# A graph network on one core: SyncE waits for the landings of gathers and counts units in place of GpSimd, and a round's weights are loaded after the first body

## The reference

```python
for l in range(L):                                   # L = 3
    agg = segment_sum(h[src], dst, num_segments=N) / deg
    logits = concatenate([h, agg], axis=-1) @ router_W[l] + router_b[l]
    ...                                              # top 2 of 8, softmax
    weak = relu(einsum('nh,ehf->nef', agg, weak_W[l]) + weak_b[l])        # 4 experts
    sh = relu(einsum('nh,ehf->nef', agg, strong_W1[l]) + strong_b1[l])    # 4 experts, 512 wide
    strong = einsum('nef,efh->neh', sh, strong_W2[l]) + strong_b2[l]
    h = h + sigmoid(h @ conf_W[l] + conf_b[l]) * einsum('ne,neh->nh', gate_dense, experts)
```

## Time and profile before

| | busy us | share of the span | instructions |
|---|---|---|---|
| TensorE (PE) | 3301.5 | 55% | 12044 |
| VectorE (DVE) | 3403.5 | 56% | 6527 |
| ScalarE (ACT) | 1200.4 | 20% | 2737 |
| GpSimd (POOL) | 4450.2 | 74% | 4528 |

### The profile page before, as it was taken

One profiled execution on the slowest core, in us unless ns is written; L12 is line 12 of the kernel. 1 busy time (PEld: TensorE's weight loads), 2 busy tenths in 40 slices (PEclk: granted clock), 3 DMA queues, 4 the chain that ended last, 5 costly groups with the idle time before them and its releaser, 6 DMA issues. The chain is left out here.

```text
span 6044.4 us, 58307 instructions
## 1 busy us (share of the span) xinstructions
PE 3301.5 (55%) x12044; PEld 2061.7 (34%) x12044; DVE 3403.5 (56%) x6527; ACT 1200.4 (20%) x2737; POOL 4450.2 (74%) x4528
## 2 busy tenths in 40 slices
PE   6249799999879899989899999100000000000000
PEld 3145455556545555565465555100000000000000
DVE  4136566663556666636566665455555536566563
ACT  1013233333223233323233333100000000000000
POOL 6767777776777777767777775777777777777777
PEclk9559899999789999979999999555555555555555
DMA  2143333333333333333333331122222212222221
GB/s 72 35 134 103 102 104 102 104 102 102 114 103 103 103 103 102 100 118 104 102 103 99 103 97 53 48 55 55 55 55 56 55 51 55 54 55 55 55 55 50
DMA packets 229761, 495.01 MB, mean 82 GB/s; under 512 B 96472, under 2 KB 113039, under 8 KB 229487
## 3 DMA queue, kind: packets, MB, share of 16 engines
q0 software_dynamic: 184432, 463.70, 28.7%
q1 hardware_dynamic: 45188, 29.87, 1.7%
HBM read 462.21 MB, written 31.05 MB: 82 GB/s over the span
## 5 line engine op out<-in xcount | busy, mean ns | idle before, releaser
L545 POOL DMA_INDIRECT ring<-hidden_tab,stage x2400 | 2330.3, 971 | 803.9 <-issue 621.6
L545 POOL DMA_INDIRECT ring<-gat_tab,stage x1600 | 1553.2, 971 | 496.5 <-issue 449.9
L834 DVE TENSOR_TENSOR ps_wide<-ps_wide,ring 128x1024 f32<-128x1024 f32 x450 | 554.7, 1233 | 335.1 <-POOLq L556 214.9
L1734 PE MATMUL ps_w1a<-ident,agg_team_t 128*128 128x128 f32 x28 | 7.8, 435 | 1044.6 <-DVE agg_team_t L1157 1044.6
L1604 PE MATMUL ps_w1a<-agg_team_t,wbuf 128*128 128x512 f32 (+1 forms) x1248 | 561.8, 572 | 7.3 <-ACT strong L1287 5.9
L1629 PE MATMUL ps_gate<-wbuf,strong 128*128 128x256 f32 x2400 | 561.5, 380 | 0.0
L1604 PE MATMUL ps_w1b<-agg_team_t,wbuf 128*128 128x512 f32 (+1 forms) x1248 | 556.0, 568 | 0.0
L1629 PE MATMUL ps_wide<-wbuf,strong 128*128 128x256 f32 x2304 | 537.2, 379 | 0.0
L1629 PEld LDWEIGHTS ps_gate<-wbuf,strong 128*128 128x128 f32 x2400 | 433.5, 191 | 111.6 <-issue 47.7
L1426 ACT ACTIVATE ps_gate<-shifted 128x36 f32<-128x36 f32 x296 | 60.4, 204 | 1959.6 <-DVEq L1068 1952.0
L1629 PEld LDWEIGHTS ps_wide<-wbuf,strong 128*128 128x128 f32 x2304 | 415.3, 190 | 78.5
(11 more groups left out here) (351 smaller groups left out, 4883.5 us busy)
## 6 DMA issues: line engine op xcount, KB each, us to landing
ring<-hidden_tab,stage POOLq DMA_INDIRECT x2400, 2.8
ring<-gat_tab,stage POOLq DMA_INDIRECT x1600, 2.6
hidden_tab<-h_res SPq DMA_DIRECT2D x12, 512.0 KB, 3.0
wbuf<-in_L_gnn_strong_W SPq DMA_DIRECT2D x6, 1024.0 KB, 9.9
wbuf<-in_L_gnn_strong_W SPq DMA_DIRECT2D x12, 512.0 KB, 12.4
wbuf<-in_L_gnn_weak_W SPq DMA_DIRECT2D x6, 512.0 KB, 7.2
stage<-slot_tab SPq DMA_DIRECT2D x125, 16.0 KB, 1.8
slot_tab<-wbuf SPq DMA_DIRECT2D x1, 1584.0 KB, 6.4
```

The lines of the kernel that those rows point to most:

```text
L545: return pool.indirect_dma_start(out=ring[:, b, 0:width], out_offset=None, in_=table, in_offset=bass.IndirectOffsetOnAxis(ap=stage[:, half ...
L834: nc.vector.tensor_tensor(wide_s, wide_s, rows(u), ALU.add).then_inc(ring_free, 1)
```

## The change

SyncE no longer follows `arrived` but makes it. For each body it waits for every unit's landing semaphore and counts the unit (`tell`); GpSimd keeps the wait for a free unit and, with it, an increment of `half_begun`, which nobody reads. Each unit is counted once, so the others wait for `u + 1` in place of `u + (r + 2)`. `round_gathered` is gone. In hidden rounds SyncE now loads the second body's indices, tells all units of the first body, issues the weights, loads the third body's indices and tells the units of the second body.

```diff
             for r in range(LAYERS + 2):
-                if r:
-                    sp.wait_ge(round_gathered, r)
                 def load(m, half):
                     return sp.dma_start(stage[:, half, :], slot_tab[:, bass.ds(m * RING, RING)]).then_inc(staged[half], 16)
-                def next_load(m, half):
+                def tell(m):
                     if r < LAYERS:
-                        sp.wait_ge(arrived, bodies * (UNITS * r) + m * UNITS + (r + 1 - 2 * UNITS))
+                        for u in range(UNITS):
+                            sp.wait_ge(gathered[u], bodies * (16 * SLOTS * r) + m * (16 * SLOTS) + 16 * SLOTS * (2 if u == UNITS - 1 else 1))
+                            sp.sem_inc(arrived, 1)
                     else:
-                        k = r - LAYERS
-                        sp.wait_ge(garrived, bodies * (GUNITS * k) + m * GUNITS + (k + 1 - 2 * GUNITS))
-                    load(m - 1, half)
+                        for u in range(GUNITS):
+                            sp.wait_ge(ggathered[u], bodies * (16 * GSLOTS * (r - LAYERS)) + m * (16 * GSLOTS) + 16 * GSLOTS * (2 if u == GUNITS - 1 else 1))
+                            sp.sem_inc(garrived, 1)
                 sp.dma_start(stage[:, 0, :], slot_tab[:, 0:RING]).then_inc(staged[0], 16)
                 if r == 0:
                     sp.wait_ge(s_slotst_rest, 16)
                 if r < LAYERS:
-                    sp.wait_ge(arrived, bodies * (UNITS * r) + (r + 1))
+                    load(1, 1)
+                    tell(0)
                     if r:
                         sp.wait_ge(w2_ready, r * BATCHES * 2 * NS)
...
-                with sp.Fori(1, bodies // 2 + 1) as j:
-                    next_load(j * 2, 1)
-                    next_load(j * 2 + 1, 0)
+                    load(2, 0)
+                    tell(1)
+                with sp.Fori(1 if r < LAYERS else 0, bodies // 2) as j:
+                    load(j * 2 + 1, 1)
+                    tell(j * 2)
+                    load(j * 2 + 2, 0)
+                    tell(j * 2 + 1)
+                with sp.Fori(bodies // 2, (bodies + 1) // 2) as j:
+                    tell(j * 2)
...
                         if b % SLOTS == SLOTS // 2:
                             pool.wait_ge(ring_free, i * UNITS + (b // SLOTS + 2))
-                            pool.wait_ge(gathered[(b // SLOTS - 1) % UNITS], i * (16 * SLOTS) + 16 * SLOTS)
-                            pool.sem_inc(arrived, 1)
+                            pool.sem_inc(half_begun, 1)
                         gather(b, half).then_inc(gathered[b // SLOTS], 16)
...
-                dve.wait_ge(arrived, first + (r + 2))
+                dve.wait_ge(arrived, first + 1)
```

More of the change, by code:

```diff
@@ L286, in gnn_kernel @@
         staged = [sem(f"staged{h}") for h in range(2)]
-        half_begun, arrived, round_gathered, ring_free, table_done = (sem(n) for n in (
-            "half_begun", "arrived", "round_gathered", "ring_free", "table_done"))
+        half_begun, arrived, ring_free, table_done = (sem(n) for n in (
+            "half_begun", "arrived", "ring_free", "table_done"))
         agg_ready, tr_ready, tr_copied = sem("agg_ready"), sem("tr_ready"), sem("tr_copied")
@@ L565, in attention_rows @@
                             pool.wait_ge(gring_free, i * GUNITS + (b // GSLOTS + 2))
-                            pool.wait_ge(ggathered[(b // GSLOTS - 1) % GUNITS], i * (16 * GSLOTS) + 16 * GSLOTS)
-                            pool.sem_inc(garrived, 1)
+                            pool.sem_inc(half_begun, 1)
                         gather(b, half).then_inc(ggathered[b // GSLOTS], 16)
@@ L577, in _ @@
                     rows(j, 0)
[L578 to L584, removed]
                 if r == LAYERS - 1:
@@ L832, in aggregate @@
                     dve.drain()
-                    dve.wait_ge(arrived, u + (r + 2))
+                    dve.wait_ge(arrived, u + 1)
                     nc.vector.tensor_tensor(wide_s, wide_s, rows(u), ALU.add).then_inc(ring_free, 1)
                 dve.drain()
-                dve.wait_ge(arrived, last + (r + 2))
+                dve.wait_ge(arrived, last + 1)
                 for b in range(SLOTS):
@@ L853, in fill_up @@
                 with dve.Fori(all_of * r + used, all_of * (r + 1)) as q:
-                    dve.wait_ge(arrived, q + (r + 2))
+                    dve.wait_ge(arrived, q + 1)
                     dve.sem_inc(ring_free, 1)
@@ L1048, in score_unit @@
                 def score_unit(unit, at):
-                    dve.wait_ge(garrived, unit + (k + 2))
+                    dve.wait_ge(garrived, unit + 1)
                     nc.vector.tensor_tensor(score[:, 0:GSLOTS, :], rows_of(unit)[:, :, GW - HEADS:GW],
@@ L1191, in _ @@
                 with dve.Fori(gall_of * k + gused, gall_of * (k + 1)) as q:
-                    dve.wait_ge(garrived, q + (k + 2))
+                    dve.wait_ge(garrived, q + 1)
                     dve.sem_inc(gring_free, 1)
```

## The result

The changed kernel takes 5999.43 us (median of 4, 5994.87 to 6000.77) against 6042.23 us of before: ratio 0.9925, interval [0.9908, 0.9942]. Two later sets of five gave 5993.9 and 5995.89 us, ratios 0.992 [0.9906, 0.9933] and 0.9918 [0.9905, 0.9932].

What follows compares the result with a forecast made beforehand. GpSimd's 4000 gathers at 1.255 us each were taken as the bound, only the excess removable: 43.8 - 3.1 - 1.7 = 39.0 us saved, other parts 0, so 6042.2 - 39.0 = 6003 us, range 5996 to 6030.

Steps and rivals of the forecast that it cites:

- the steps: GpSimd's landing stalls removed, by round: 11.8, 11.7, 11.2, 2.0 and 2.3 us saved, 39.0 us together.
- the sum: Landing stalls of 43.8 us, minus 3.1 and 1.7 that shorten nothing: 39.0 us saved, all other parts at 0.
- Its own range: Narrower range of the forecast alone, 5998 to 6012 us: at most 43.8 or 47.8 us saved, at least 30.
- Round 2: The third hidden round: 13.1 us of GpSimd's landing stalls over the normal gap, of which 11.2 us would be saved.
- a growth of over 3 us a round: Sign of a wrong prediction: GpSimd's waits for a free ring unit at L829 growing by more than this.
- Rival 2: TensorE sets the pace, savings turn into full-ring waits in hidden rounds: 6030 to 6038 us, chance 0.07.
- SyncE as the counter: A wait and an increment a unit on SyncE: at most 2 us over 11 critical places, taken as 0.
- The weights' place: Weights issued behind the first body of each hidden round, landing at 66 us of the round: cost 0.
- the cover: Spare time before late weights cost anything: TensorE's team 0 may start at about 84 us, weights land at 66: 18 us.
- Rival 3: Weights and stage load too late at the third body's first gather and TensorE's team 0: 6054 us or more, chance 0.05.
- Rival 1: The first body's stall returns as longer gathers or a full descriptor store in the second body: 6028 us, chance 0.10.
- Rival 4: Stalls at the third gather wait for a free unit, not a landing, and stay: 6042 us; 0.06 including the unseen.

Runs made afterwards that it cites:

- the two later kernels: The changed kernel with the weights issued after 12 units and after 16 units instead of 8: 6026.75 us (ratio 0.9967) and 6084.86 us (ratio 1.0064).

## Why the prediction was right

**The mechanism** was: GpSimd at 1.255 us a gather, and only the excess can go. The idle for landings went entirely: "issue" is 0.305 us per gather in every round, and the gathers themselves are unchanged. By rounds, from first gather to next first gather, the profile gives 12.4, 12.8, 8.9, 4.9 and 7.0 us (0.8 lost ahead of round 0); the steps were 11.8, 11.7, 11.2, 2.0 and 2.3.

**What was missing** is a term of the sum: the waits of L578 to L584. The removed code stood in the diff, and the prediction counted the landing waits inside the loop alone. They were 4.04 and 4.47 us where 0.30 is normal, 7.9 us together; the experiment that puts them back measures 7.8. With them the sum is 46.9 us, 5995, and the three sets lie at 5994 to 5999. So the saving was 8 us too small in the working, and the forecast is 4 to 9 us above the three medians; that it is only 4 above the first is in part luck. Its own range had a slip too: at most 47.8 us saved would give 5994 us as its lower end, not 5998. The same waits in hidden rounds would have been counted at nothing, and rightly.

**Round 2** was put at 11.2. Three profiled executions of the changed kernel give 8.9, 12.2 and 15.5 against the one profile of before, so neither too high nor too low can be said. The row that could make it smaller was in the prediction: 14.7 us of waits for a free ring at L829. These waits grew by 7.0, 3.8 and 1.0 us; the prediction expected 0.4 for round 2, and named a growth of over 3 us a round as a sign that it was wrong. In the first execution the part of the round ahead of team 2 counts fully (9.2 us), and the rest of it gives nothing. Rival 2 can thus be true in part for one round in three; how large the part is stays open.

**SyncE as the counter** was taken at no cost, and costs none that can be seen: a count follows its landing within 0.1 us, where the profile tells the landing, units 8 and 9 apart, which are counted at 55 to 56 us behind the weights' issues. VectorE waits 402.1 us for it in the attention rounds, where it waited 404.8 for GpSimd, and less in the hidden rounds (387.4 against 433.0).

**The weights' place** was taken at no cost, right, and shown by the kernel that leaves them at the start. But two numbers in the working were wrong. They landed at 62 to 63 us, not 66. And the cover was given as 18 us, from TensorE's idle before team 2; the ring is the nearer limit. VectorE takes up the second group of team 1 some 32 us after TensorE's start of team 0, and gathers fit only until 108 us of the round (the third gather of unit 21 is preceded by 86: 86 x 1.255), so about 75 us is the last start without cost, 74 by the two later kernels: cover 12 us from the weights' 62. Rival 3 thus had the right mechanism, a late team 0, with the wrong limit: neither stage nor the crowding was it. It also assumed 279 GB/s as all there is. From the first issue of the weights to their last landing, the DMA engines moved more after the change; the second row is the same stretch in the kernel that issues them at the start of the round (us, busy of PE, PEld, DVE, ACT, POOL, clock, DMA share, GB/s):

```profile
1527.80:1549.00 21.20, 10.10 (x49) 10.01 (x48) 9.24 (x15) 2.42 (x8) 16.02 (x18) 0.50 0.97 354
...
1489.24:1518.00 28.76, 28.76 (x150) 28.76 (x150) 6.78 (x13) 8.47 (x19) 21.31 (x23) 0.54 0.86 279
```

At the start of the round rival 3's 30 us for the weights comes out nearly; in the second body it does not.

The prediction weighed a rule of the Trainium skill against the change: *DMA: Bandwidth & Descriptors*, "Queues, rings and completion order", has the queues take turns, packet by packet. The runs agree in direction. Beside gathers that GpSimd does not hold back the weights take longer than beside gathers that it holds back: 21 us against 19 in the second body (the changed kernel and the one with only the weights moved), 27 to 29 against 23 to 24 at the start of the round. But that did not make them late, and no gather landed later than 5.9 us after its issue in this execution (7.1 in the last set's). Rival 1 fell too: of the gathers issued while the weights were under way in the second body none took over 0.96 us. Rival 4 fell with the landing waits.

## What to carry to other kernels

An engine that sets the pace by issuing DMAs one after the other should not be the one that waits for them; give the wait and the count to an engine with nothing else to do, and leave the issuer only the wait for room. What can be gained is the idle over the normal gap, not the number of waits, and every wait of the removed kind must be looked up, those behind the loops too. For a transfer that is moved later, the deadline can be the first buffer that fills behind it: here a start of team 0 at 74 us, where the idle of the engine that reads the weights would have allowed 84.

## What the runs showed of the hardware

- 5.24 MB of weights took 21 us from the first issue to the last landing in the second body (354 GB/s with the gathers, DMA engines 0.97 busy), but 27 to 29 us at the start of the round with GpSimd not waiting for landings either (279 GB/s, 0.86 busy). Why the start is slower isn't known.
- Some of VectorE's instructions hold up a GpSimd gather that starts while they run. In the changed kernel's profile 115 of the 4000 gathers took over 1 us, and 111 of them, the two of 6.7 us too, ended 0.82 to 0.86 us after such an instruction had ended. These instructions read two operands from SBUF: the product of 6.89 us, the sum L865 and five more. Beside the sum L833 and the product L1078, which read one of their operands from PSUM, no gather was held; 250 and 229 gathers began there with over 0.5 us of the instruction still to run and kept their 0.95 us. Nor were 22 gathers that began within 0.04 us of the start of L865. The 115 gathers add up to 72 us over the normal, more than this change saves; how much of it is time of the kernel was not measured, but for the product cut in seven. A held gather and the sum beside it:

```profile
484.76 1.98 POOL L553 DMA_INDIRECT ring<-hidden_tab,stage  x1 [0.30 <-issue]
...
484.69 1.23 DVE L865 TENSOR_TENSOR h_res<-h_res,x_res 128x1024 f32<-128x1024 f32 x1
```

- A semaphore wait and a count on GpSimd between two gathers cost nothing when the landing is in time: before the change 0.305 us stand ahead of a gather with them and ahead of one without.
